# Exponentials of turned scores made and released per PSUM bank in three narrow attentions

## The reference

```python
x = x + tanh(g_xattn[0]) * attn(layernorm(x), ctx, mask=key mask,  L0 weights)
x = x + tanh(g_ffn[0])   * experts(layernorm(x))
...                                          # layer 1
x = x + tanh(g_xattn[2]) * attn(layernorm(x), ctx, mask=pair mask, L2 weights)
...
x = x + tanh(g_xattn[3]) * attn(layernorm(x), ctx, no mask,        L3 weights)
...
# attn, per batch and head (d_k = 8):
scores = q @ k.T / sqrt(8)                   # 128 queries x 128 keys, 16 heads
attn   = softmax(scores + mask, axis=-1)
out    = (attn @ v) @ Wo.T + bo              # layer 3 sums the heads before Wo
```

## Time and profile before

| what | us |
|---|---|
| median of 3 runs | 1837.81 (1837.2 to 1841.56) |
| the profiled execution's own time | 1836.88 |
| its span, first to last instruction | 1835.0 |
| PE busy in the span | 1713.5 (93%) |
| ACT busy in the span | 870.3 (47%) |

### The profile page before, as it was taken

The page is one execution under the profiler, slowest core; times in us unless marked ns, Lnnn a source line. Parts: engine busy times, 40 slices in busy tenths (PEclk is TensorE's granted clock), DMA queues, the critical chain, the costliest instruction groups (busy, mean ns, idle before and its releaser), DMA issues. The chain is left out here.

```text
span 1835.0 us, 46859 instructions
## 1 busy us (share of the span) xinstructions
PE 1713.5 (93%) x17896; PEld 1094.8 (60%) x17896; DVE 1097.2 (60%) x2372; ACT 870.3 (47%) x2183; POOL 638.9 (35%) x1075
## 2 busy tenths in 40 slices
PE   5999989899999999978987999979999989999898
PEld 2555554577777777655765444436777765555454
DVE  5677667566566665654166777763222236777576
ACT  3555426455555555534443444434434336454354
POOL 4466519223223232211121455500000004666573
PEclk9999999999999999999998999979999999999999
DMA  4000041000000000010101000000000010000000
GB/s 114 2 3 3 2 118 35 9 7 7 5 7 5 7 7 5 2 47 12 35 0 52 3 3 3 3 1 1 1 0 0 0 36 13 2 3 2 2 24 23
DMA packets 47823, 27.66 MB, mean 15 GB/s; under 512 B 11024, under 2 KB 44560, under 8 KB 47632
## 3 DMA queue, kind: packets, MB, share of 16 engines
q1 hardware_dynamic: 42896, 24.64, 4.7%
q10 hardware_dynamic: 4736, 0.35, 0.2%
HBM read 22.88 MB, written 2.10 MB: 14 GB/s over the span
## 5 line engine op out<-in xcount | busy, mean ns | idle before, releaser
L837 DVE TENSOR_REDUCE neg_max<-scores 128x8 f32<-128x1024 f32 x192 | 235.0, 1224 | 131.6 <-PE scores L579 45.9
L2049 ACT ACTIVATE probs<-scores,neg_max 128x128 f32<-128x128 f32 x512 | 182.3, 383 | 190.0 <-DVE neg_max L2107 190.0
L1911 POOL TENSOR_TENSOR probs<-probs,inverse 128x512 f32<-128x512 f32 x128 | 133.0, 1039 | 335.1 <-DVE inverse L2115 334.9
L547 PE MATMUL scores<-k_diag,q_all 32*128 32x512 f32 x768 | 217.0, 642 | 6.5 <-ACT k_all L706 4.4
L561 PE MATMUL turned<-q_diag,k_all 32*128 32x512 f32 x768 | 216.4, 637 | 0.5 <-ACT probs L748 0.5
L748 ACT ACTIVATE probs<-turned 128x1024 bf16<-128x1024 f32 (+1 forms) x128 | 131.0, 1023 | 172.6 <-PE turned L593 172.6
L432 POOL TENSOR_TENSOR k_diag<-k_all,hmask 128x512 f32<-128x512 f32 x96 | 99.9, 1042 | 318.7 <-ACT k_all L706 290.5
L1569 ACT ACTIVATE hidden_f<-hb_f,b_f 128x512 f32<-128x512 f32 x128 | 87.8, 687 | 129.0 <-PE hb_f L1515 128.8
L1524 PEld LDWEIGHTS yb_f<-w_f,hidden_f 128*128 128x128 f32 x1024 | 119.2, 192 | 14.8 <-issue 14.8
L1524 PE MATMUL yb_f<-w_f,hidden_f 128*128 128x128 f32 x1024 | 119.3, 275 | 0.0
L2107 DVE TENSOR_REDUCE neg_max<-scores 128x8 f32<-128x1024 f32 x64 | 78.4, 1224 | 68.3 <-PE scores L1960 68.3
(11 more groups left out here) (326 smaller groups left out, 3707.5 us busy)
## 6 DMA issues: line engine op xcount, KB each, us to landing
ctx_t<-in_ctx_t_dram SPq DMA_DIRECT2D x24, 256.0 KB, 3.0
w_f<-in_L_ffn_W_dram SPq DMA_DIRECT2D x16, 256.0 KB, 3.1
x_state<-in_x_dram SPq DMA_DIRECT2D x4, 512.0 KB, 8.1
ctx_t<-in_ctx_t_dram SPq DMA_DIRECT2D x16, 128.0 KB, 2.1
out_dram<-x_state SPq DMA_DIRECT2D x7, 256.0 KB, 2.3
w_f<-in_L_ffn_We_dram SPq DMA_DIRECT2D x1, 1024.0 KB, 7.1
taps_f<-in_L_ffn_conv_w_dram SPq DMA_DIRECT2D x1, 768.0 KB, 6.4
y_weights_or_value_parts<-_ffn_expert_weights_dram SPq DMA_DIRECT2D x1, 512.0 KB, 4.3
```

Of the source, the lines that this page charges most:

```text
L547: last = nc.tensor.matmul(scores[pair][:, (g % 2) * 512:(g % 2 + 1) * 512], cols(q_all, b, S)[quad_rows(g), :], k_diag[quad_rows(g), b % 2 ...
L837: v.tensor_reduce(neg_max[:, b % 2, 8 * pair:8 * pair + 8], scores[pair][:, :].rearrange("p (h k) -> p h k", k=S), axis=X_AXIS, op=ALU.max ...
L1911: nc.gpsimd.tensor_tensor(p4, p4, inverse[:, n % 2, CH * h:CH * h + CH].unsqueeze(2).to_broadcast([P, CH, S]), ALU.mult).then_inc(s["prob_ ...
L2049: last = nc.scalar.activation(probs[:, n % 2, h, c * S:(c + 1) * S], scores[n % 2][:, i * S:(i + 1) * S], ACT.Exp, bias=neg_max[:, n % 2, ...
```

## The change

The exponential of a pair, one instruction on 1024 columns, becomes two on 512 columns, one per bank, each with its own wait and its own release. `shifts` releases st_done after each of its two matmuls instead of after the second. `crosswise` waits before each of its two matmuls for the exponential of that bank in the filling before, instead of once for the whole. The counts of the other waits on these semaphores are doubled. Nothing else is changed.

```diff
@@ queries_apart
-                wait(pool, s["st_done"], 2 * b - 2)
+                wait(pool, s["st_done"], 4 * b - 4)
@@ crosswise
-                wait(pe, s["exp_done"], 2 * b + pair)
                 for g in (2 * pair, 2 * pair + 1):
+                    wait(pe, s["exp_done"], 4 * b + g - 1)
                     nc.tensor.matmul(turned[:, (g % 2) * 512:(g % 2 + 1) * 512], cols(k_all, b, S)[quad_rows(g), :],
@@ shifts
                     last = nc.tensor.matmul(turned[:, (g % 2) * 512:(g % 2 + 1) * 512], ones_b[quad_rows(g), :],
                                             shift[quad_rows(g), b % 2, :], start=False, stop=True, skip_group_check=tiled)
-                last.then_inc(s["st_done"], 1)
+                    last.then_inc(s["st_done"], 1)
@@ contexts
-                pe.wait_ge(s["exp_done"], 2 * b + 2)
+                pe.wait_ge(s["exp_done"], 4 * b + 4)
@@ exponents
-                act.wait_ge(s["st_done"], 2 * b + pair + 1)
                 wait(act, s["sums_done"], b - 1)
                 bias = {"bias": key_cols[:, b:b + 1]} if mask == "keys" else {}
-                nc.scalar.activation(probs[:, b % 2, pair, :], turned[:, :], ACT.Exp, **bias).then_inc(s["exp_done"], 1)
+                for half in (slice(0, 512), slice(512, 1024)):
+                    act.wait_ge(s["st_done"], 2 * (2 * b + pair) + half.start // 512 + 1)
+                    nc.scalar.activation(probs[:, b % 2, pair, half], turned[:, half], ACT.Exp, **bias).then_inc(s["exp_done"], 1)
@@ copy_shift
-                wait(act, s["st_done"], 2 * b - 2)
+                wait(act, s["st_done"], 4 * b - 4)
```

## The result

| what | before | after |
|---|---|---|
| median of 7 runs each, us | 1838.76 (1837.2 to 1841.56) | 1843.04 (1841.49 to 1849.53) |
| profiled execution's own time, us | 1836.88 | 1843.01 |
| its span, us | 1835.0 | 1841.1 |
| ratio after/before | | 1.003, 95% interval 1.0017 to 1.0043 |

The changed kernel is slower by 0.30%, with an interval that lies above no change (the medians alone give 0.23%). The forecast was +1.0 us; the medians differ by 4.3, the profiled executions by 6.1. The 1843.0 us lie near the upper end of the whole range (1834.5 to 1844) and outside the forecast's own (1836.5 to 1841).

What follows compares the result with a forecast made beforehand. The prediction saw a loop through exponential, crosswise, masks and shifts as the bound in layers 0 and 2, PE's queue in layer 3. Terms 1.4 - 1.2 + 0.5 + 0.3 = +1.0 us gave 1838.8 us, range 1834.5 to 1844.

Steps and rivals of the forecast that it cites:

- What bounds the kernel: Layers 0 and 2: a loop of exponential, crosswise, masks, shifts; layer 3: PE's queue decides at the pair-0 place, 1.26 us.
- Two instructions for one: ACT's exponential: cutting it adds a fixed cost, +0.15 us in layer 0 (1.26), +0.07 in layers 2 and 3 (1.09).
- Rival 2: ACT: halves don't overlap, taking 1.20 and 1.36 to 1.37 us; +13.4 us, 1851.2 us; chance 0.11.
- The estimate from the Trainium skill's figures: ACT's cut, from a fixed part of 186 or 280 ns and about 93 ns overlap: +4.8 us, 1842.6 us.
- The waits of crosswise: PE: first matmul free everywhere; second sets the period, released 1.31 us (layer 0) or 1.14 (layers 2, 3) after exponential's start.
- rival 3: Layer 2's first crosswise matmul: its head start is worth time, up to -14 us, 1824 us; chance 0.05.
- An earlier start of the exponential: ACT: lower bank complete earlier starts the exponential 0 to 0.01 us sooner per filling, 0.01 taken at half the places.
- The sum: Layer 0 pair-0 +1.4, layer 2 pair-0 -1.2 and pair-1 +0.5, layer ends +0.3: +1.0 us, 1838.8 us.
- Rival 1: ACT: the cut costs more, halves overlap by 0.05 us, taking 1.14 and 1.31; +5.6 us, 1843.4 us; chance 0.14.
- Rival 4: Later stages: a shift may move where clock drops fall, 3 us on either side; chance 0.08.

Runs made afterwards that it cites:

- quarters: The changed kernel with ACT's wait order mended and each half exponential made in two again, four instructions of 256 columns: 1862.32 us, ratio 1.0122.
- the order mended: The changed kernel with the exponential's wait for st_done written ahead of its wait for sums_done again: 1837.26 us, ratio 0.9996.
- the cut alone: The kernel before with the exponential made in two halves, but waited for and released once: 1844.57 us, ratio 1.0039.

## Why the prediction was wrong, point by point

- *What bounds the kernel*: right. Layer 0 and 2 are set by the loop through the exponential, layer 3 by PE; the places and their lengths (1.27, 1.17, 1.11) carry every experiment. Layer 3's steady steps are 5.34 us in all kernels but the quarters' (5.35).
- *Two instructions for one*: right to the hundredth, 1.26 to 1.27 and 1.08 to 1.09 after. Rival 2 (no overlap, +13.4) did not happen. The estimate from the Trainium skill's figures ("ScalarE: Activation LUTs", section "What ACT_TABLE_LOAD costs"), 0.09 and 0.19 for the cut, is a little over what is measured, 0.06 and 0.15.
- *The waits of crosswise*: right. The second matmul is free 0.05 after its half, and the first one's head start gives nothing; rival 3 is refuted.
- *An earlier start of the exponential*: this is the step that failed. The prediction took a gain of 0.01 us at half of the places, 0 to 0.01 as the bounds, "and nothing hides here that could be lost". Measured is a loss of 0.05 at every place: 0.50 against 0.45, 0.48 against 0.43. With the order mended it is the forecast's gain, 0.44 and 0.42. The steps that the prediction named tell the same: layer 2's was to stay within 0.03 of 5.98 and is 6.07, layer 0's was to grow by about 0.04 and grew by 0.11. The prediction counted the two releases and left out the edit in the same lines that writes `wait(act, s["sums_done"], b - 1)` ahead of the other wait. The rows had a price of this kind: 0.14 against 0.05 on PE for a wait that stands apart and one that doesn't, read from the earlier trace rows, and used for `crosswise` alone. A smaller miss is hidden: in layer 0's pair-0 filling the two shift matmuls lie 0.53 - 0.38 = 0.15 apart, not 0.01, since the crosswise ones ahead of them do. The bank that is early by it gains nothing, because PE's own queue sets the pair-1 place behind it.
- *The sum*: 1.4 - 1.2 + 0.5 + 0.3 = +1.0 us holds for the kernel with the order mended. From the start of a layer's first exponential to the start of its last, layer 0 took 184.56 us before and takes 185.95 there, +1.39 (forecast +1.4); layer 2 took 195.90 and takes 195.05, -0.85 (forecast -1.2 + 0.5 = -0.7); layer 3 stays within 0.1. That the profiled spans differ by +1.2 agrees, but single spans also differ by parts that these layers don't make, and the medians have -0.8. The changed kernel, with the missing term, takes 187.74 and 198.60 us in the same way: 1.8 us more than with the order mended in layer 0, where only the pair-0 place feels the later start (31 x 0.06), and 3.5 in layer 2, where with halves both places do, together 5.3 us. The profiled spans have 1841.1 - 1836.2 = 4.9. Layer 3's exponentials start later too, but PE's queue sets its steps. Beside this lie single delays of 0.3 us, one step in layer 2 and two in layer 3 of the changed kernel's trace; where they come from is open.
- *Rival 1* gave +5.6 us, about the measured size, for another reason. A size that fits shows no cause: the halves are no longer than forecast.
- *Rival 4*: the clock doesn't explain the loss. Its mean over the profiled spans is 0.982 before and 0.983 after, and the steps are longer in stretches where it is 1.00. But runs of one kernel lie 3 to 8 us apart, so that a loss of 5 can't be told from single runs.

## What to carry to other kernels

Where an instruction needs two semaphores, try writing first the wait that comes last. Here the other order cost 0.06 us on ACT, and 0.09 on PE until the second matmul, every time, and where the loop passes through that instruction it came to about 5 us on either engine. When a change is read, the order of waits is part of it, also where the set of waits is the same. Cutting an instruction so that a consumer can start on its first part didn't pay here: both parts ran side by side on PE, the last part was all that counted, and it got free 0.04 us later in layer 0 and only 0.03 earlier in layer 2.

## What the runs showed of the hardware

- Of two waits ahead of one exponential or crosswise matmul, the one written first is carried by it. The other stands in the trace as an instruction of its own: 180 times at L748 in the changed kernel, one of them at 124.38 us on ACT, and the exponential starts at 124.45. With the order mended the wait for st_done has none, and L29 has 666 again. The Trainium skill says in "Perfetto Trace Analysis", section "Identifying Dependency Chains", that instructions waiting on several engines may get such instructions ahead of them; the trace agrees, and the runs add the price.
- A stall behind such a separate wait was shown as "issue" (20 at L561, 4.6 us) in the kernel before, and not at all in the changed one; with the wait on the instruction, 20 stalls (3.3 us) appear with their releaser.
- Two neighbouring exponentials overlap by 0.10 us though the second has a wait of its own: two of 0.60 take 1.09, as without that wait in the cut alone. Whether they would if that wait were still open, no row shows.
- The crosswise matmuls, on different 32 rows of the array, neither slow each other nor gain from a head start: the masks follow the second crosswise matmul by 1.05 us whether the first began beside it or 0.4 us ahead.
